# Inverse sums in one tile, and a fused attention and mixture kernel's orders and banks laid out anew

## What is computed

```
a = layernorm(x)                          # over the 64 channels
bias[h,i,j] = a[i,j,:] @ Wb[:,h]          # one bias for all rows r
q, k, v = a @ Wq, a @ Wk, a @ Wv
p = softmax_j(q.k / sqrt(32) + bias + mask)
x1 = x + ((p @ v) * sigmoid(a @ Wg)) @ Wo
t  = layernorm(x1)
e  = top2 of softmax(t @ router_w + router_b), renormalised
out = x1 + sum_e e * (t @ expert_w[e] + expert_b[e])
```

## Time and profile before

| what | value |
| --- | --- |
| median of 3 runs | 878.78 us |
| the profiled execution | 878.26 us, span 876.5 us |
| PE / DVE / POOL / ACT busy | 802.0 / 753.1 / 644.2 / 500.5 us |
| granted clock of PE | 0.971 of full speed on average |
| first phase and begin of the steps | until about 97 us |
| last exponent of a group (group 39) | 813.5 us |

### The profile page before, as it was taken

The page is one execution under the profiler, slowest core; times in us unless marked ns, Lnnn a source line. Parts: engine busy times, 40 slices in busy tenths (PEclk is TensorE's granted clock), DMA queues, the critical chain, the costliest instruction groups (busy, mean ns, idle before and its releaser), DMA issues.

```text
span 876.5 us, 40872 instructions
## 1 busy us (share of the span) xinstructions
PE 802.0 (92%) x15532; PEld 534.2 (61%) x15532; DVE 753.1 (86%) x1818; ACT 500.5 (57%) x1049; POOL 644.2 (74%) x1029
## 2 busy tenths in 40 slices
PE   1999679999999999999999999999999999999643
PEld 1899345666666666666666666666666666666411
DVE  8998545899999999999899998999999999998754
ACT  3887245655665566655665566655565566665220
POOL 6995002487788877887788878888788877888786
PEclk9999999999999999999999999999999999999955
DMA  4563100111110100101011100101011100100000
GB/s 118 193 200 137 39 25 22 37 39 35 34 56 30 37 30 30 52 30 37 30 45 37 37 30 30 52 30 37 30 44 38 37 30 30 52 25 18 17 15 16
DMA packets 32461, 40.82 MB, mean 47 GB/s; under 512 B 6288, under 2 KB 27280, under 8 KB 32400
## 3 DMA queue, kind: packets, MB, share of 16 engines
q1 hardware_dynamic: 31920, 39.95, 14.0%
q10 hardware_dynamic: 480, 0.02, 0.0%
HBM read 13.74 MB, written 6.55 MB: 23 GB/s over the span
## 4 chain that ended last, share of the span: by engine, by line
PE 67%; POOL 11%; issue 10%; DVE 9%; ACT 2%; DMA 0%; POOLq 0%; DVEq 0%
PE psS L1117 11%; PE psS L1092 6%; PE psS L1124 5%; DVE rinv L841 3%; POOL ln_s L375 3%; PE ps_x L1174 3%; PE ps_m L1174 3%; PE psS L1136 2%; PE ps_x L1177 2%; PE psS L1097 2%; PE ps_m L1177 2%; PE ps_o L1249 2%; POOL xn L378 2%; PE ps_x L1148 2%; PE ps_x L1250 2%
## 5 line engine op out<-in xcount | busy, mean ns | idle before, releaser
L825 DVE TENSOR_REDUCE negm<-psS 128x12 f16<-128x1920 f32 x80 | 145.7, 1821 | 16.2 <-PE psS L1097 9.0
L428 POOL TENSOR_TENSOR add<-prod 128x256 f32<-128x256 f32 x160 | 116.9, 730 | 4.3 <-DVE prod L943 2.1
L375 POOL TENSOR_TENSOR ln_s<-ln_s,half 128x5 f32<-128x5 f32 (+1 forms) x60 | 86.2, 1436 | 37.1 <-DVE ln_s L881 29.7
L433 POOL TENSOR_TENSOR add<-add 128x128 f32<-128x128 f32 x200 | 92.0, 460 | 3.1
L394 POOL TENSOR_TENSOR xc<-x,ln_s 128x320 f32<-128x320 f32 x40 | 29.3, 731 | 87.9 <-DVE ln_s L874 87.9
L545 ACT ACTIVATE pt_a<-psS 128x1280 f32<-128x1280 f32 x40 | 49.5, 1238 | 67.5 <-PE psS L1126 67.5
L545 ACT ACTIVATE pt_b<-psS 128x1920 f32<-128x1920 f32 x40 | 70.8, 1771 | 13.8 <-PE psS L1136 13.7
L435 POOL TENSOR_TENSOR ymix<-add 128x64 f32<-128x64 f32 x200 | 64.1, 321 | 15.7
L1092 PE MATMUL psS<-bm,ident 128*128 128x480 f16 (+1 forms) x320 | 68.0, 335 | 6.6 <-ACT pt_b L545 2.1
L416 POOL TENSOR_TENSOR og_lo<-og,og_hi 128x320 f16<-128x320 f32 x80 | 63.4, 793 | 10.5 <-ACT og_hi L582 9.9
L1117 PE MATMUL psS<-bt_hi,ident 128*128 128x320 f16 (+1 forms) x320 | 67.7, 334 | 3.3 <-issue 2.6
(11 more groups left out here) (267 smaller groups left out, 2921.2 us busy)
## 6 DMA issues: line engine op xcount, KB each, us to landing
xin<-in_x SPq DMA_DIRECT2D x20, 320.0 KB, 3.0
xs_all<-xs_pair SPq DMA_DIRECT2D x20, 320.0 KB, 2.5
xs_q<-xs_all SPq DMA_DIRECT2D x40, 160.0 KB, 2.1
xs_v<-xs_all SPq DMA_DIRECT2D x40, 160.0 KB, 2.1
xin<-in_x SPq DMA_DIRECT2D x40, 160.0 KB, 2.2
out<-res SPq DMA_DIRECT2D x40, 160.0 KB, 1.8
w_raw<-in_expert_w SPq DMA_DIRECT2D x2, 128.0 KB
eb_raw<-in_expert_b SPq DMA_DIRECT2D x15, 2.0 KB
```

The lines of the kernel that those rows point to most:

```text
L375: pool.tensor_tensor(ln_s[a][:, 3, 0:w], ln_s[a][:, 2, 0:w], half[:, 0:w], ALU.pow).then_inc(own, 1)
L428: pool.tensor_tensor(add1[t % 2][:], prod_of(t)[:, 0:4, :], prod_of(t)[:, 4:8, :], ALU.add).then_inc(mix_step[t], 1)
L433: pool.tensor_tensor(add2[t % 2][:], add1[t % 2][:, 0:2, :], add1[t % 2][:, 2:4, :], ALU.add).then_inc(mix_step[t], 1)
L825: dve.tensor_reduce(negm[c][:, :, 0:slots], psS[:, :, 0:slots * N].rearrange("i h (s j) -> i h s j", s=slots), AX.X, ALU.max, negate=True) ...
```

## The change

The row sums are now made twice, in partitions 32 h + r and 32 h + 4 + r, by ones in four more columns of `row_one` and `rest_one`. ACT makes two tiles of the reciprocals: `rinv_s`, rounded to float16, negative in the first four partitions of a head and positive in the others, and `rinv_u`, float32, zero in the first four. POOL's one subtraction `rinv_u - rinv_s` gives `rinv_hl`: the high half in the first four partitions, the low half in the next four. `row_to_all` has ones for both sets, so one matmul spreads both halves. The loop of the steps is gone: all steps are written out on all engines. And the lists of PE, ACT, DVE and POOL have a new order, with other small banks for many calls.

```diff
-        rinv_hi = sb("rinv_hi", [P, N], F16)
-        rinv_lo = sb("rinv_lo", [P, N], F16)
+        rinv_s = sb("rinv_s", [P, N], F16)
+        rinv_u = sb("rinv_u", [P, N])
+        rinv_hl = sb("rinv_hl", [P, N], F16)
+        sign, upper = sb("sign", [P, 1]), sb("upper", [P, 1])
...
-            for n in range(FIRST, LOOP):
-                step(n, n % 2)
-            pairs_loop(eng, step, LOOP, LOOP_END)
-            for n in range(LOOP_END, LAST):
+            for n in range(FIRST, LAST):
                 step(n, n % 2)
...
+            for first in (0, -RG):
+                if first: pool.wait_ge(const_ready, N_CONST - 1)
+                pool.affine_select(out=row_to_all[:].rearrange("p r (h e) -> p r h e", h=H),
+                                   in_=row_to_all[:].rearrange("p r (h e) -> p r h e", h=H),
+                                   compare_op=ALU.not_equal, fill=0.5 / SUM_UP, base=first,
+                                   pattern=[[-1, RG], [-DH, H], [0, DH]], channel_multiplier=1).then_inc(const_ready, 1)
...
             def rinv_low(g):
                 pool.wait_ge(rh_done, g + 1)
-                pool.tensor_tensor(rinv_lo[:], rinv[:], rinv_hi[:], ALU.subtract).then_inc(rl_done, 1)
+                for c in range(2):
+                    need(pool, rb_done[c], g)
+                pool.tensor_tensor(rinv_hl[:], rinv_u[:], rinv_s[:], ALU.subtract).then_inc(rl_done, 1)
...
             def rinv_high(g):
                 act.wait_ge(rinv_done, g + 1)
-                for c in range(2):
-                    need(act, rb_done[c], g)
-                act.activation(rinv_hi[:], rinv[:], ACT.Copy).then_inc(rh_done, 1)
+                need(act, rl_done, g)
+                act.activation(rinv_s[:], rinv[:], ACT.Copy, scale=sign[:, 0:1])
+                act.activation(rinv_u[:], rinv[:], ACT.Copy, scale=upper[:, 0:1]).then_inc(rh_done, 1)
...
             def mask_tables():
+                prep(dve.tensor_reduce(upper[:], fold[:, 0:RG], AX.X, ALU.add))
+                prep(dve.tensor_scalar(sign[:], upper[:], -2.0, 1.0, ALU.mult, ALU.add))
+                prep(dve.tensor_scalar(upper[:], upper[:], -1.0, 1.0, ALU.mult, ALU.add))
...
                 for s in range(2):
-                    mm(o, lhsT=row_to_all[:, 2 * c + s, :], rhs=rinv_hi[:], start=True, stop=False)
-                    end = mm(o, lhsT=row_to_all[:, 2 * c + s, :], rhs=rinv_lo[:], start=False, stop=True)
+                    end = mm(o, lhsT=row_to_all[:, 2 * c + s, :], rhs=rinv_hl[:], start=True, stop=True)
```

More of the change, by code:

```diff
@@ L197, in pairs_loop @@
                 body(i * 2 + (first + 1), 1 - first % 2)
[L199 removed]
+        N_MEMSET, N_CONST = 18, 24
         TAIL = 4
@@ L631, in step @@
                 b = 1 - a
-                if on(n): keep_v_rest(n, a, ps_r)
-                if on(n + 1): tanh_gate(n + 1, b, 1, ps_x)
+                if on(n - 1): rinv_high(n - 1)
+                if on(n - 2): og_high(n - 2, 1)
+                if on(n): exponent(n, a, 0)
+                if later(n + 1): qk_high(n + 1, b, 0, 0, ps_m)
+                if on(n): keep_m(n, a, 1, ps_r)
+                if on(n): keep_v_rest(n, a, ps_o)
+                if on(n - 4): keep_coef(n - 4, banks16[2])
+                if on(n + 1): tanh_gate(n + 1, b, 1, ps_m)
                 if on(n - 3): router_exp(n - 3)
-                if on(n - 1): rinv_high(n - 1)
-                if on(n - 3): keep_expert(n - 3, 2, ps_x)
+                if on(n + 1): tanh_gate(n + 1, b, 0, ps_r)
+                if on(n - 3): keep_expert(n - 3, 2, ps_m)
                 if on(n - 2): square2(n - 2, a)
-                if on(n + 1): tanh_gate(n + 1, b, 0, ps_r)
                 if on(n): exponent(n, a, 1)
+                if on(n - 2): high2(n - 2, a)
+                if later(n + 2): qk_high(n + 2, a, 1, 0, ps_o)
                 if on(n): keep_v(n, a, ps_m)
-                if on(n - 2): high2(n - 2, a)
-                if later(n + 2): qk_high(n + 2, a, 1, 0, ps_m)
-                if on(n - 1): og_high(n - 1, 1)
-                if on(n + 1): keep_m(n + 1, b, 0, ps_r)
+                if on(n + 1): keep_m(n + 1, b, 0, ps_m)
                 if on(n - 2): keep_xs2(n - 2, a, banks16[0])
@@ L648, in step @@
                 if later(n + 2): qk_high(n + 2, a, 1, 1, ps_x)
-                if on(n + 1): exponent(n + 1, b, 0)
-                if later(n + 2): qk_high(n + 2, a, 0, 0, ps_m)
-                if on(n - 3): keep_coef(n - 3, banks16[0])
-                if on(n + 1): keep_m(n + 1, b, 1, ps_r)
             run_steps(act, step)
@@ L956, in step @@
                 b = 1 - a
-                if on(n - 2): normed(n - 2, 1, ps_r)
-                if on(n - 4): weigh(n - 4, 0, ps_x)
-                if on(n - 4): weigh(n - 4, 1, ps_o)
                 if on(n - 2): normed(n - 2, 0, ps_r)
                 if on(n): row_max(n, 1)
-                if later(n + 1): qk_low(n + 1, b, 1, 0, ps_m)
+                if later(n + 1): qk_low(n + 1, b, 1, 0, ps_o)
                 if on(n - 1): invert(n - 1, ps_x)
+                if on(n - 4): weigh(n - 4, 3, ps_r)
                 if on(n - 4): share(n - 4, 6)
-                if on(n - 4): weigh(n - 4, 3, ps_r)
-                if on(n - 4): share(n - 4, 7)
+                if later(n + 1): qk_low(n + 1, b, 0, 1, ps_m)
                 if on(n - 3): logits(n - 3, ps_o)
@@ L969, in step @@
                 if on(n - 3): route(n - 3, 2)
-                if later(n + 1): qk_low(n + 1, b, 0, 1, ps_m)
+                if on(n - 4): share(n - 4, 7)
                 if on(n - 3): route(n - 3, 3)
@@ L977, in step @@
                 if on(n - 3): route(n - 3, 7)
+                if later(n + 1): qk_low(n + 1, b, 0, 0, ps_m)
                 if on(n - 3): route(n - 3, 8)
                 if on(n - 1): gated(n - 1, b, 1, ps_x)
-                if later(n + 1): qk_low(n + 1, b, 0, 0, ps_m)
                 if on(n - 3): route(n - 3, 9)
                 if on(n - 3): route(n - 3, 10)
+                if on(n - 3): route(n - 3, 11)
                 if on(n + 1): row_max(n + 1, 0)
-                if on(n - 3): route(n - 3, 11)
+                if on(n - 1): gated(n - 1, b, 0, ps_x)
                 if on(n - 3): route(n - 3, 12)
@@ L992, in step @@
                 if on(n + 1): rest_max(n + 1)
-                if on(n - 1): gated(n - 1, b, 0, ps_m)
                 if on(n - 3): share(n - 3, 4)
+                if on(n - 3): share(n - 3, 5)
                 if on(n - 2): sumsq2(n - 2, a)
-                if on(n - 3): share(n - 3, 5)
-                if on(n - 4): finish(n - 4, a, ps_m)
+                if on(n - 1): normed(n - 1, 1, ps_m)
+                if on(n - 4): finish(n - 4, a, ps_r)
+                if on(n - 3): weigh(n - 3, 1, ps_o)
+                if on(n - 3): weigh(n - 3, 0, ps_x)
             run_steps(dve, step)
@@ L1267, in step @@
                 b = 1 - a
-                if not isinstance(n, int) or n == LOOP_END:
-                    last[id(psS)] = max_done[1], n + 1
-                    last[id(ps_o)] = lg_done, n - 2
-                    last[id(ps_r)] = prod_done[3], n - 3
-                    last[id(ps_m)] = qkl_done[0][1], n + 2
-                    last[id(ps_x)] = qkl_done[1][1], n + 2
                 if on(n): scores(n, a, 0)
```

55 lines of the change are left out of this document (25 added, 30 removed).

## The result

The changed kernel takes **869.73 us** (median of four runs, 867.04 to 871.18), where the kernel before took 878.88 (878.75 to 879.07) beside it: ratio 0.9891, 95% interval 0.9869 to 0.9912. The forecast was 868.6, range 864 to 875. A second set of four runs of the same kernel gave 869.24 (869.19 to 870.42) and 0.9892.

A forecast was written before the change was run, and what follows sets the result against it. PE was taken as nearly gapless, waiting for the reciprocal and barely covered by the exponent at psS. 3.0 + 4.5 + 2.5 + 0.85 - 0.6 = 10.2 us off gave 868.0 against the profiled execution, 868.6 for the median; range 864 to 875.

The forecast's parts named there:

- The thin cover at psS: Between scores(n, 1) and max_scores(n + 1, 1), the exponent hides PE's work: 0.085 of 0.28 us gained a step, 3.0 off.
- Rival 1: All of the spread's saving on PE arrives, 0.28 us a step: 861.8 us; chance 7%.
- Steps written out: Loop removed: 30 steps of 17.83 us without turns, 4.5 us off, fetching taken as 0.
- Rival 3: Written-out steps don't pay: fetching costs as much as the turn did, 0.15 us a step: 873.1 us; chance 8%.
- Hand-overs (a) to (d): New waits between engines from moved calls and banks, those that PE meets; counted as costing nothing.
- rival 2: A new hand-over or exponent(n, 1) is 0.1 to 0.2 us late in every step: 874.3 us; chance 17%.
- (c): project_v in ps_m waits for normed(n - 1, 1), done some 0.2 us ahead of need; no cost.
- (d): gated(n - 1, 0) ahead of attention_out on DVE: mean 0.14 us later, square2 still 0.41 ahead of exponent(n, 1).
- Rival 4: Slower: on ACT, square2 ahead of exponent(n, 1) comes late through DVE's mean; 885.3 us if 0.85 later; chance 8%.
- (e), project_v_rest: On PE, moved from in front of attend 0 to behind attend 1: -0.05 to +0.04 us a step, taken as 0.
- The drain: After step 38 POOL sets the pace; weigh_kept moves into its idle time: 2.5 us off, bounds 0 and 3.5.
- The begin: Step -1: project_qk(1, 0, 1) waits for m_t instead of k_lo, 0.85 us off; mask_tables' three DVE instructions, 0.6 on.

The follow-up runs named there:

- a_exp_heads: after with exponent(n, 1) split into two instructions of two heads each, the first letting max_scores(n + 1, 1) begin; 861.69 us, ratio 0.9799.
- b_noloop: The kernel before with all steps written out instead of the loop, nothing else changed; 874.78 us, ratio 0.9955.
- after: The changed kernel, with the whole change against the kernel before; 869.73 us, ratio 0.9891.
- a_heads_finish: a_exp_heads with expert_bias ahead of spread_inverse(n - 1, 1) on PE and finish ahead of normed(n - 1, 1) on DVE; 866.54 us, ratio 0.9848.
- a_kept_late: after with POOL's weigh_kept put back behind norm2 and mix_halves(n - 3, 0); 879.49 us, ratio 1.0002.
- after_again: after, unchanged, run and profiled once more; 869.24 us, ratio 0.9892.

## Why the prediction was right, step by step

- **The thin cover at psS** was right to about 0.02: 0.085 a step forecast, 0.074 measured alone (0.047 with the loop kept) and 0.064 when undone, with a wait of 0.194 as the price. The other sign of being wrong did not come either: the exponent into pt_b starts 0.04 after the last matmul of scores ends, before and after. Rival 1, all of the 0.28, would have needed 17.55 a step; that came only when a_exp_heads took the exponent out of the way (17.543). Both halves of the argument are shown by that: the exponent was the cover, and nothing else lay close behind.
- **Steps written out**: 4.5 forecast, 3.7 measured by b_noloop. The term was mis-sized: it took every step as 17.83, and the written-out steps are 17.83 and 17.88 in turn. Rival 3 (0.15 a step) falls. By the 108 ns that the Trainium skill, Advanced Engine Details and Errata, section Control Flow Timing, gives for a compare-and-branch, 15 turns are an estimated 1.6 us; 0.25 us were paid for one turn here, and what the rest of a turn is made of no run shows. The Trainium skill, Runtime: NRT & Kernel Launch, section Instruction fetch mechanics, says that straight code is fetched ahead. This case agrees: with the loop gone there are 125 packets for 43, and the mean step is 0.12 us shorter.
- **Hand-overs (a) to (d)**: none is paid, as forecast, and rival 2 falls for after. (b) is 0.1 of turn2 inside the reciprocal's wait. (c) was near its limit, as a_heads_finish showed by crossing it. For (d) the row of square2 stands here, whose end is 0.41 ahead of the exponent at 294.35, the spare that the prediction had left. Rival 4 falls with it:

```profile
293.47 0.47 ACT L598 ACTIVATE sq<-xc 128x320 f32<-128x320 f32 x1 [0.99 <-POOL xc L395]
```

- **(e), project_v_rest**: taken as 0 between -0.05 and +0.04. It is -0.03 to -0.04, some 1.2 to 1.6 us off. A term that was mis-sized, within its bounds.
- **The drain**: 2.5 forecast, 2.2 measured between the profiles. POOL's rows in after (before: the earlier trace rows):

```profile
841.89 1.18 POOL L376 TENSOR_TENSOR ln_s<-ln_s,half 128x5 f32<-128x5 f32 x1
...
854.81 1.04 POOL L425 TENSOR_TENSOR kept<-kept,coef 128x512 f32<-128x512 f32 x1 [0.71 <-DVE coef L934]
856.36 0.72 POOL L431 TENSOR_TENSOR add<-prod 128x256 f32<-128x256 f32 x1 [0.51 <-DVE prod L950]
```

  Counted from the last exponent, the second of the two powers of the drain came 35.16 us later before and 34.58 now, so the first step gave 0.6 (forecast 0.4) and the rest 1.6 (forecast 2.1). Not all of it is the order's: the old order's other four profiles have a drain of 62.2 to 62.3, 0.65 shorter than that of before, with the loop and without; why, no run tells. So the order's own share is 1.5. What the step missed is that weigh_kept matters in the steps too; it was costed only where it gains. In the drain its place is worth 3.3 (a_kept_late), of which the rest of the order takes 1.8 back.
- **The begin** is the step that failed: 0.25 off forecast, 1.84 on measured. The wait of project_qk(1, 0, 1) in step -1 shrank as foreseen, from 1.55 us behind k_lo to 0.59 behind m_t:

```profile
106.74 0.45 PE L1088 MATMUL ps_m<-xs_q,w_hi 128*128 128x320 f16 x1 [0.59 <-ACT m_t L572]
```

  The three instructions of mask_tables cost 0.54 (forecast 0.6), and the first phase itself was some 0.7 later in this profile than in that of before: together the 1.21 by which max_scores(0, 1) starts later, 103.74 for 102.53. In after_again the first phase was 0.6 earlier than in before, and the row starts at 102.49. The other 0.63 came behind it, in both profiles, although a wait had shrunk there by 1: before's profile ran at 2.4 GHz from 102.5 to about 104 and again from about 108.5, after's at 1.2 until about 111.5, and that ate the gain. The prediction took the begin's times from one profile as if they were the kernel's.
- **The sum**: by the marks of the experiments 3.7 + 2.6 + 1.2 = 7.5 off in the steps and 1.5 (the order's share) to 2.2 in the drain: 9.0 to 9.7 off. Against 878.9 to 879.3 that is 869.2 to 870.3, with the begin as it falls; the runs say 869.2 and 869.7. That the forecast came this near is in part luck: it had the turns 0.8, the spread 0.4 and the drain 0.3 to 1.0 too high and project_v_rest 1.2 too low, and these nearly cancel. The lower end of its own bounds, 864.5, does not come out of the terms named for it: 1.9, 1 and 0.4 below 868.6 are 865.3.

## What to carry to other kernels

Before costing work that an edit removes, find the next instruction of that engine which waits for another engine, and read how long it would have to wait if the work were gone: only the cover's thickness is gained, here 0.07 of 0.28 us, and the rest comes free only when that other engine's release comes sooner (split it by bank). When orders on several engines change together, undo each alone: one of them may be what pays for another, in every step and not only where it was costed. And times of a begin with idle gaps on PE are to be read from several profiles, never from one.

## What was not expected of the hardware

- From max_scores(0, 1) to the first exponent the same work took 12.95 us or 15.98, by PE's level. Two profiles of one kernel had their first exponents 1.25 us apart, and there the level was the same and the first phase differed.
- The column of the granted clock does not show this. In before it falls to 0.50 between 106 and 108 us; in after it reads 1.00 over all of the begin, also in the stretch below, where matmuls of 320 columns start 0.26 apart. The spacing tells the level:

```profile
104.00:106.00 2.00, 2.00 (x16) 0.85 (x14) 0.57 (x1) 0.00 (x0) 0.00 (x0) 1.00 0.00 0
```

- An exponent of 128 x 1920 split in two costs 0.06 us in all, 1.83 for 1.77, so cutting an instruction to release its reader sooner is nearly free on ACT.
